# A looped program for TensorE in a routed attention, and the normalisation one slot later

## What is computed

```python
x = x + tanh(g_xattn[0]) * L0_xattn(layernorm(x), ctx, ctx, ...)     # rope on keys and values
x = x + tanh(g_ffn[0])   * L0_ffn(layernorm(x), ...)                 # 8 experts, top 2, and a shared one
x = x + tanh(g_xattn[1]) * L1_xattn(layernorm(x), ctx, ctx, mask, ...)
x = x + tanh(g_ffn[1])   * L1_ffn(layernorm(x), ...)                 # gated gelu feed-forward
x = x + tanh(g_xattn[2]) * L2_xattn(layernorm(x), ctx, ctx, mask, ...)
x = x + tanh(g_ffn[2])   * L2_ffn(layernorm(x), ...)                 # fp8 matmul
x = x + tanh(g_xattn[3]) * L3_xattn(layernorm(x), ctx, ctx, ...)
x = x + tanh(g_ffn[3])   * L3_ffn(layernorm(x), ...)                 # 8 experts, top 2

# an attention, 16 heads of 8 channels
q, k, v = heads(h @ Wq.T + bq), heads(ctx @ Wk.T + bk), heads(ctx @ Wv.T + bv)
w = softmax(q @ k.T / sqrt(8));  out = merge(w @ v) @ Wo.T + bo
# the router of the last layer
probs = softmax(h @ router_w.T);  top_v, top_i = top_k(probs, 2)
```

## Time and profile before

| | |
|---|---|
| median of 3 runs | 3282.54 us (3276.01 to 3284.56) |
| profiled execution | 3298.21 us, its span 3296.4, mean granted clock 0.886 |
| PE busy | 2532.8 us (77% of the span) |
| DVE, ACT, POOL busy | 1566.6 (48%), 1380.2 (42%), 978.3 us (30%) |
| chain of work that ended last | PE 11%, DMA 5%, DVE 5%, PE's own issue 4%, ACT 1%, POOL 1% |

### The profile page before, as it was taken

How to read it: one execution, slowest core, us unless ns; L and a number is a source line. 1 busy time by engine, 2 the same in 40 slices (tenths; PEclk the granted TensorE clock), 3 DMA queues, 4 the chain that set the end, 5 groups by cost and what they waited for, 6 DMA issues and landing times. The chain is left out here.

```text
span 3296.4 us, 74894 instructions
## 1 busy us (share of the span) xinstructions
PE 2532.8 (77%) x28202; PEld 1794.6 (54%) x28202; DVE 1566.6 (48%) x4283; ACT 1380.2 (42%) x1992; POOL 978.3 (30%) x1052
## 2 busy tenths in 40 slices
PE   4888864439997799989999969993288777358883
PEld 2555543328886455567777735551145444247773
DVE  3555544424443577622222247776667665513322
ACT  2555533213332466644545436661055444124441
POOL 4444426634444112110000000001112433634444
PEclk9999976669999899989999979996599888679997
DMA  3010101126665222100000011110011111146666
GB/s 98 22 24 20 23 16 38 39 80 195 197 192 153 78 53 61 34 3 0 0 0 0 1 44 45 41 41 11 11 32 31 37 35 37 44 144 191 189 186 219
DMA packets 143775, 219.56 MB, mean 67 GB/s; under 512 B 27177, under 2 KB 94513, under 8 KB 143026
## 3 DMA queue, kind: packets, MB, share of 16 engines
q1 hardware_dynamic: 96930, 90.25, 10.8%
q10 hardware_dynamic: 29232, 90.37, 8.8%
q0 software_dynamic: 17408, 36.21, 3.2%
HBM read 157.48 MB, written 43.61 MB: 61 GB/s over the span
## 5 line engine op out<-in xcount | busy, mean ns | idle before, releaser
L1541 DVE TENSOR_REDUCE mx<-psS 128x16 f32<-128x1024 f32 x264 | 322.6, 1222 | 321.9 <-PE psS L1096 294.1
L650 POOL DMA_INDIRECT yg<-ysb,yidx x288 | 279.5, 970 | 421.0 <-DVE ysb L2005 190.6
L470 POOL TENSOR_TENSOR ve<-mv,eps 128x4 f32<-128x4 f32 x102 | 20.3, 199 | 1184.4 <-DVE mv L1517 1182.3
L756 ACT ACTIVATE work<-psT 128x1024 f32<-128x1024 f32 x260 | 266.2, 1024 | 215.5 <-PE psT L1105 214.8
L750 ACT ACTIVATE work<-work 128x1024 f32<-128x1024 f32 x264 | 278.3, 1054 | 135.9 <-DVE work L1543 132.7
L1096 PE MATMUL psS<-kexp,qT 64*64 64x512 f32 x2112 | 307.6, 634 | 31.0 <-DMA kexp<-kT 15.3
L1543 DVE TENSOR_TENSOR work<-psS,mx 128x1024 f32<-128x1024 f32 x264 | 323.2, 1224 | 9.1
L1105 PEld LDWEIGHTS psT<-ident,work 128*128 128x128 f32 x2080 | 239.6, 145 | 151.5 <-issue 99.8
L1105 PE MATMUL psT<-ident,work 128*128 128x128 f32 x2080 | 288.3, 283 | 5.3 <-ACT work L756 3.3
L1381 PEld LDWEIGHTS psY<-w_ffn,work 128*128 128x128 f32 x2016 | 247.8, 192 | 9.4 <-DVE work L1976 1.2
L1381 PE MATMUL psY<-w_ffn,work 128*128 128x128 f32 x2016 | 248.5, 275 | 1.6 <-DVE ysb L1999 1.0
(11 more groups left out here) (278 smaller groups left out, 4645.0 us busy)
## 6 DMA issues: line engine op xcount, KB each, us to landing
w_ffn<-in_wmoe ACTq DMA_DIRECT2D x72, 578.0 KB
w_ffn<-in_wmoe ACTq DMA_DIRECT2D x72, 576.0 KB
ctxT<-in_ctxT SPq DMA_DIRECT2D x76, 256.0 KB, 2.8
xin<-xg SPq DMA_DIRECT2D x144, 132.0 KB
kexp<-kT SPq DMA_DIRECT2D x1152, 16.0 KB
gio<-yg SPq DMA_DIRECT2D x16, 512.0 KB, 3.9
work<-yg SPq DMA_DIRECT2D x16, 512.0 KB, 6.4
yg<-ysb,yidx POOLq DMA_INDIRECT x288
```

The costliest lines, as they stand in the source:

```text
L650: e.indirect_dma_start(out=yg, out_offset=bass.IndirectOffsetOnAxis(ap=yidx[:, b, t:t + 1], axis=0), in_=ysb[:, b, t, :], in_offset=None, ...
L756: e.activation(pT[:, s % 2, :], psT[:, :], ACT.Copy).then_inc(pt_ok, 1)
L1541: e.tensor_reduce(mx[:, :], src, AX, ALU.max).then_inc(s_max, 1)
```

## The change

It has five parts.

1. PE's program of attention 3 has turns 4 to 13 as a loop of two turns with five iterations; turns 0 to 3 and 14 to 19 stay written out. The other engines' programs of that attention stay written out.
2. A loop of two turns can't name one of four ring buffers, so `apply` on DVE writes the rows to a new buffer `xnf`, from which PE transposes. It waits for the previous chunk's transposes (`xt_ps`).
3. POOL gets the step `rows`: four `tensor_scalar` of 128x128 a turn, which compute the same rows once more into the ring, between x_bias and scatter. `scatter` and DVE's `stats` wait for it (`nrm`).
4. `macc` has one buffer, and `counts` waits for the ranks' matmuls that read it (`rank_ps`).
5. In all four attentions `normalise` of turn u−1 comes behind the first shift of turn u on DVE, and in slot 0 `v_proj` comes ahead of `weigh` on PE.

```diff
@@ -140,2 +140,3 @@
         ring.append(gio3[:, :, :])
+        xnf = sb("xnf", [P, LT, D])
         lgt = sb("lgt", [P, GT * E])
@@ -564,2 +565,12 @@
 
+def rows(c):
+    b = (c % 2) * LT
+    if c >= 8 and c % 2 == 0:
+        e.wait_ge(m[f"sd{c // 2 % 4}"], 16 * 2 * GT * (c // 8))
+    e.wait_ge(m["rstd"], c + 1)
+    for t in range(LT):
+        mm = e.tensor_scalar(ring[c // 2 % 4][:, b + t, 0:D], xs(None, c, t), mmv[:, b + t, 0:1],
+                             mrstd[:, 1, b + t:b + t + 1], ALU.subtract, ALU.mult)
+    mm.then_inc(m["nrm"], 1)
+
 def scatter(g, c):
@@ -567,2 +578,3 @@
         e.wait_ge(m["seq"], MSTEPS[lay] * (g + 1))
+        e.wait_ge(m["nrm"], 2 * g + 2)
     for t in range(GT):
@@ -583,2 +595,4 @@
         x_bias(lay, None, u)
+    if 2 <= u < CHUNKS + 2:
+        rows(u - 2)
     if u >= 6 and u % 2 == 0:
@@ -1169,5 +1183,5 @@
         p_turn(lay, i, *ahead(u, s, 1))
-        weigh(lay, i, u, s)
         if s == 0:
             v_proj(lay, i, u + 1)
+        weigh(lay, i, u, s)
         if s == 2:
@@ -1190,11 +1204,11 @@
 
-def turn_x(c):
-    e.wait_ge(m["xn"], c + 1)
-    e.wait_ge(x_up, K0 + lay * CHUNKS + c + 2 if c + 2 <= CHUNKS else K0 + (lay + 1) * CHUNKS)
+def turn_x(i, u):
+    e.wait_ge(m["xn"], val(i, u, 1, -2))
+    e.wait_ge(x_up, val(i, min(u, CHUNKS + 1), 1, K0 + lay * CHUNKS - 1))
     for t in range(LT):
-        mm = e.transpose(psX[:, t * P:(t + 1) * P], ring[c // 2 % 4][:, c % 2 * LT + t, 0:D], ident[:, :])
+        mm = e.transpose(psX[:, t * P:(t + 1) * P], xnf[:, t, :], ident[:, :])
     mm.then_inc(m["xt_ps"], 1)
 
-def route(c):
-    e.wait_ge(m["xt_sb"], c + 1)
+def route(i, u):
+    e.wait_ge(m["xt_sb"], val(i, u, 1, -2))
     for t in range(LT):
@@ -1203,4 +1217,7 @@
 
-def rank(g):
-    e.wait_ge(m["seq"], MSTEPS[lay] * g + 18)
+def group(i, u, per, plus):
+    return per * ((u - 5) // 2) + plus if i is None else i * per + (per * ((u - 5) // 2) + plus)
+
+def rank(i, u):
+    e.wait_ge(m["seq"], group(i, u, MSTEPS[lay], 18))
     out8 = psX[:, GT * E:2 * GT * E].rearrange("p (t x) -> p t x", t=GT)
@@ -1210,3 +1227,3 @@
                  start=False, stop=False, skip_group_check=True)
-    e.matmul(out8, ones16[:, :], macc[:, lay // 3, g % 2, :].rearrange("p (a x) -> p a x", a=1)
+    e.matmul(out8, ones16[:, :], macc[:, lay // 3, 0, :].rearrange("p (a x) -> p a x", a=1)
              .broadcast_to([P, GT, E]), start=False, stop=True).then_inc(m["rank_ps"], 1)
@@ -1224,34 +1241,44 @@
 p_turn(lay, None, 0, 0)
-for u in range(CHUNKS + 4):
+
+def turn(i, u):
     inside = u < CHUNKS
-    c = u - 3
+    routed = 3 <= u < CHUNKS + 3
+    ranked = u >= 5 and u % 2 == 1
     for s in range(LT):
         if inside:
-            scores(lay, None, *ahead(u, s, 2))
+            scores(lay, i, *ahead(u, s, 2))
         if s == 1 and inside:
-            q_proj(lay, None, u + 1)
-        if s == 1 and 0 <= c < CHUNKS:
-            turn_x(c)
-        if s == 2 and 0 <= c < CHUNKS:
-            route(c)
-        if s == 3 and 0 <= c < CHUNKS:
-            e.wait_ge(m["lg"], c + 1)
-        if s == 3 and u >= 5 and u % 2 == 1:
-            rank((u - 5) // 2)
+            q_proj(lay, i, u + 1)
+        if s == 1 and routed:
+            turn_x(i, u)
+        if s == 2 and routed:
+            route(i, u)
+        if s == 3 and routed:
+            e.wait_ge(m["lg"], val(i, u, 1, -2))
+        if s == 3 and ranked:
+            rank(i, u)
         if inside:
-            p_turn(lay, None, *ahead(u, s, 1))
-        if s == 3 and u >= 5 and u % 2 == 1:
-            e.wait_ge(m["rk"], (u - 5) // 2 + 1)
+            p_turn(lay, i, *ahead(u, s, 1))
+        if s == 3 and ranked:
+            e.wait_ge(m["rk"], group(i, u, 1, 1))
         if s == 3 and u + 2 <= CHUNKS:
-            ln_t(ATT[lay], None, u + 2)
-        if inside:
-            weigh(lay, None, u, s)
+            ln_t(ATT[lay], i, u + 2)
         if s == 0 and inside:
-            v_proj(lay, None, u + 1)
+            v_proj(lay, i, u + 1)
+        if inside:
+            weigh(lay, i, u, s)
         if s == 2 and inside:
-            k_proj(lay, None, u + 2)
+            k_proj(lay, i, u + 2)
         if s == 3 and 0 < u <= CHUNKS:
-            out_proj(lay, None, u - 1)
+            out_proj(lay, i, u - 1)
+
+for u in range(4):
+    turn(None, u)
+with e.Fori(0, (CHUNKS - 6) // 2) as i:
+    turn(i, 4)
+    turn(i, 5)
+for u in range(CHUNKS - 2, CHUNKS + 4):
+    turn(None, u)
 e.wait_ge(m["seq"], MSTEPS[lay] * (NG - 1) + 20)
-e.matmul(psO[:, 0:E], ones16[:, :], macc[:, lay // 3, NG % 2, :], start=True, stop=True).then_inc(m["cnt_ps"], 1)
+e.matmul(psO[:, 0:E], ones16[:, :], macc[:, lay // 3, 0, :], start=True, stop=True).then_inc(m["cnt_ps"], 1)
 
@@ -1597,2 +1624,4 @@
         if s == 0:
+            if i is not None or u >= 1:
+                normalise(lay, i, u - 1)
             if lay == 1 and u + 2 < CHUNKS:
@@ -1607,3 +1636,2 @@
             ln_apply(ATT[lay], i, u + 2)
-    normalise(lay, i, u)
 
@@ -1616,2 +1644,3 @@
 turn(None, CHUNKS - 1)
+normalise(lay, None, CHUNKS - 1)
 x_update(lay, None, CHUNKS - 2)
@@ -1648,2 +1677,3 @@
         e.wait_ge(m["xn"], c - 1)
+        e.wait_ge(m["nrm"], c - 1)
     for t in range(LT):
@@ -1657,4 +1687,4 @@
     b = c % 2 * LT
-    if c >= 8 and c % 2 == 0:
-        e.wait_ge(m[f"sd{c // 2 % 4}"], 16 * 2 * GT * (c // 8))
+    if c >= 1:
+        e.wait_ge(m["xt_ps"], c)
     e.wait_ge(m["rstd"], c + 1)
@@ -1662,3 +1692,3 @@
     for t in range(LT):
-        mm = e.tensor_scalar(ring[c // 2 % 4][:, b + t, 0:D], xs(None, c, t), mmv[:, b + t, 0:1],
+        mm = e.tensor_scalar(xnf[:, t, :], xs(None, c, t), mmv[:, b + t, 0:1],
                              mrstd[:, 1, b + t:b + t + 1], ALU.subtract, ALU.mult)
@@ -1706,3 +1736,4 @@
     step(e.tensor_reduce, mcol[:, 8, :], mask16[:, :, :].rearrange("p t x -> p x t"), AX, ALU.add)
-    step(e.tensor_tensor, macc[:, lay // 3, (g + 1) % 2, :], macc[:, lay // 3, g % 2, :], mcol[:, 8, :], ALU.add)
+    e.wait_ge(m["rank_ps"], g + 1)
+    step(e.tensor_tensor, macc[:, lay // 3, 0, :], macc[:, lay // 3, 0, :], mcol[:, 8, :], ALU.add)
 
@@ -1742,2 +1773,4 @@
         if s == 0:
+            if 1 <= u <= CHUNKS:
+                normalise(lay, None, u - 1)
             if 2 <= u < CHUNKS + 2:
@@ -1769,4 +1802,2 @@
                 shifted(gn)
-    if inside:
-        normalise(lay, None, u)
```

More of the change, by code:

```diff
@@ L1247, in attention_routed @@
+                        if s == 0 and inside:
+                            v_proj(lay, i, u + 1)
                         if inside:
-                            weigh(lay, None, u, s)
-                        if s == 0 and inside:
-                            v_proj(lay, None, u + 1)
+                            weigh(lay, i, u, s)
                         if s == 2 and inside:
-                            k_proj(lay, None, u + 2)
+                            k_proj(lay, i, u + 2)
                         if s == 3 and 0 < u <= CHUNKS:
-                            out_proj(lay, None, u - 1)
+                            out_proj(lay, i, u - 1)
```

## The result

The changed kernel takes 3297.59 us (median of 5 runs, 3294.64 to 3301.58), the kernel before 3282.54 (5 runs, 3276.01 to 3284.56): ratio 1.0053, 95% interval 1.0039 to 1.0067, slower by 15 us. The forecast was 3294, slower by 11.3.

What follows compares the result with a forecast made beforehand. Scatter bursts that stop PE for most of 12 us were taken to bound attention 3's burst turns. −3.5 + 5 × 1.0 + 5 × 1.56 + 1.96 = +11.3 us gave 3294 us, range 3258 to 3324.

Steps and rivals of the forecast that it cites:

- Slower by 11.3: Whole kernel: the sum of all terms, +11.3 us, for a median of 3294 us.
- The loop, 0 and not a relief: PE's loop in attention 3: gains nothing in the bursts, taken as 0, bounds 0 to +3.5 us.
- E: Rival, attention 3's loop: each taken branch waits 2.8 us for its first page, +14 on the sum, 3308; chance 0.01.
- B: Rival, attention 3's bursts: a resident loop ends PE's stall, 8 × 8.5 = −68 us, 3226; chance 0.13.
- Odd turns +1.56: Odd burst turns of attention 3: POOL's rows delay the burst by 1.96 us, the reorder gives −0.4.
- +1.0 of even turns: Even burst turns of attention 3: DVE has no slack, so the gates that release the scatters come later, +1.0 us.
- Rows at 0.49 us: POOL's four new 128x128 tensor_scalar in attention 3: 0.49 us each, four 1.96, bounds 0.94 to 5.1.
- rival D: POOL becomes the bound in attention 3: row instructions cost 1.28 us each, +40, 3322; decides from 0.78 us; chance 0.19.
- Attention 1, 0 with bounds ±0.15 a turn: Reorder in attention 1: q_proj at 1275.1 instead of 1274.98, +0.1, taken as 0 a turn.
- Attention 0, 0 with bounds to +8: Reorder in attention 0: taken as 0; up to +8 us, 0.5 a turn, if weighing behind the shift delays k_proj.
- −0.7 a turn in attention 3: Reorder in attention 3, turns 1 to 5: q_proj at 2447.4 instead of 2448.12, −3.5 us in all.
- C: Rival, attention 3: POOL's rows fit into waits, DVE's slip is made up; −0.7 × 15 turns = −10.5, 3272; chance 0.17.

Runs made afterwards that it cites:

- loop_no_order: The changed kernel with the old order of normalise and v_proj in all attentions; 0.9988 of the kernel before.
- between_unrolled: The changed kernel with one POOL row instruction behind every second scatter and PE's loop in attention 3 written out; 0.9938 of the kernel before.
- norm_later: The kernel before with normalise alone moved behind the next turn's first shift, weigh still ahead of v_proj; 1.0256 of the kernel before.
- rows_no_loop: The kernel before with xnf, POOL's rows and the single macc, PE written out, old order; 1.0006 of the kernel before.
- v_first: The kernel before with v_proj alone moved ahead of weigh, normalise still at the turn's end; 1.0052 of the kernel before.

## Why the prediction was right, and where not

- *Slower by 11.3* came out as slower by 15, and that it fits is luck: by the traces the turns with bursts lost 11.6 us less than forecast, and everything else 11.8 more.
- *The loop, 0 and not a relief*: right. No transfer of q8 in 245 us and yet PE back 12.2 us after a burst's start; a loss of 10 us or more (E) falls in loop_no_order, a gain as large as B's there and in between_unrolled.
- *Odd turns +1.56*: wrong. The step that failed is "in odd turns POOL waited only 0.16: all of it delays the burst" and that a later burst is a later everything. The odd burst was delayed, by 2.0 us in the mean though the rows cost 3.3, and PE's ranks got out ahead of the hold; the next interval was 1.8 us shorter. A pair grew by 0.25 us where I had 2.56, which takes in the +1.0 of even turns. That early ranks are what gives the delay back is argued, with one sign for it within a single trace: in norm_later, on a chip with long holds, the even burst follows 33.7 us behind the odd one whose ranks were out after 4.1 us, and 34.5 to 35.8 behind the three whose ranks took 11.7. rows_no_loop, on a chip with short holds, costs 2 us in all.
- *Rows at 0.49 us*: mis-sized, 0.82 measured. It passed the 0.78 at which rival D decided, and D's sign, no wait for DVE in even turns, is in the trace. D's price isn't, for the reason above. Only the tail paid in full, 3.5 us for 1.96.
- *Attention 1, 0 with bounds ±0.15 a turn*: wrong size, +0.34. The count to q_proj gave +0.1; the waits on PE up to there cost 0.17, and the rest is the `xn` that a POOL instruction stretches from 0.34 to 1.12 us, which wasn't in it.
- *Attention 0, 0 with bounds to +8*: 3.5, inside, but not by k_proj, whose waits didn't grow (9.2 and 7.6 us in 200:400). PE's granted clock went from 0.97 to 0.93 behind the waits of v_proj's second half, which became longer.
- *−0.7 a turn in attention 3*: right in turns with the router's work (19.94 for 20.56), but 0 to −0.2 in plain ones, and turn 5 gave it back.
- C's gain and my loss are both real, on different chips. Nothing in the trace of before said that its 12 us holds belonged to the chip as much as to the program. Each chip was seen in one session only, so whether it is the chip or its state at that time is open.

What in the pauses lets PE go on is not shown. The runs show that it does, on the chip where the hold is long: gaps gone in the timeline, more matmuls in a burst, shorter pairs.

## What to carry to other kernels

A wait that is moved off one step is to be followed round the whole turn on every engine, to the last step that the loop carries, not to the step that it freed; and look at what the other engines run at its new time. Where a stall of fixed length is started by one engine, a delay of the start is no cost in itself: ask what gets out ahead of it. And instructions that an engine has to run anyway are well placed between its scatters.

## What the hardware showed unexpectedly

- While eight indirect DMAs run one after the other on POOL, TensorE's issue and what it gives to others are held up, on the first chip until 2.1 to 2.2 us behind the burst's end (10.07 us from its start). How much differed by chip: turns with bursts took 30.7 us on the first (29.4 in v_first on the fourth) and 24 in the kernel before on the third (22.4 to 23.6 in four kernels on the second), and the kernel before 3282 and 3278 against 3210 and 3212. The sign of this change turned with it (1.0053 and 0.9979).
- Where the hold is long, a pause of 0.8 us behind every second scatter nearly doubles the matmuls that run in an even burst, from 6 to 11 a us.
- A `tensor_scalar` of 128x128 on DVE that starts 0.24 us behind a `tensor_tensor` of 128x512 on POOL takes 1.12 us instead of 0.34 and ends just behind POOL's. In attention 1 the reorder brought the two together in nearly every turn.
- A reorder can cost clock: in attention 0 eight waits of TensorE of 2.1 us in the mean, instead of 1.85, came with a granted clock of 0.93 for 0.97 over 200 us.
- `tensor_scalar` with two column operands on 128x128 takes 0.82 us on POOL, where 128x4 with constants takes 0.24 and a `tensor_tensor` of 128x512 1.28. POOL's cost isn't one of size alone.
